# The last batch of a mixer kernel: only its last mixer in halves, and the router's mean summed by TensorE

## The chip, the cores and the metric

One core of a Trainium2 chip runs the whole kernel. The metric is device time in microseconds of one launch, the median over runs.

## The reference

The input x is 8 batches of 1024 tokens by 256 channels, float32. For each batch:

```python
n = layernorm(x)
logits = n @ gate_W                      # 4 mixers, the best 2 with softmax weights: comb
for m in 4 mixers:
    g, v, d = n @ Wg[m] + bg[m], n @ Wv[m] + bv[m], n @ Wd[m] + bd[m]
    h[m] = linear_scan(sigmoid(g) * tanh(v), a=0.001 + 0.998 * sigmoid(d))   # along the tokens
t = x + layernorm(sum_m comb[m] * h[m])
u = layernorm(t)
z = batchnorm(mean of u * ln_g + ln_b over the tokens)
expert, gate = argmax and max of softmax(z @ Wr + br)     # one of 8 experts per batch
y = (relu(u' @ W_down[expert] + b) @ W_up[expert] + b) * gate    # u' = u * ln_g + ln_b
out = t + layernorm(y)
```

(The reference's own names for the shapes of the expert part are larger; it runs on the same 8 batches.) The scan is serial over the 1024 tokens; everything that follows the mean over all tokens (the expert) needs the whole batch.

## The kernel before

Channels lie on the partitions for the products and scans, tokens for the normalisations. A batch has 8 planes (mixer m, half of the channels); a plane has 2 chunks of 512 tokens and 3 kinds (gate, decay, value), so a batch has 48 banks. Each bank is 6 float16 products of 128 x 512 (high and low parts of x and of the weights; `product`, L1196) into one of three PSUM banks, which ACT evacuates with sigmoid or tanh (`evacuate`, L535; L541 maps the decay). VectorE multiplies gate and value (L830), scans a plane (L806) and adds the mixers up (`combine`, L823) from transposed states: TensorE's float32 transposes `turn_h` (L1206). `a_moments`, `residual` and `t_moments` (statistics at L704) lead to t, with a power on POOL (L429) for each root; `scale_t` (L740, L743) gives factor and shift of each token, and the rows normalised by ACT (L571) or VectorE (L756) are turned by `turn_u` (L1159) and split into fp16 halves by ACT (`high_u`, L548, which also sums them over the tokens by accumulation) and VectorE (`low_u`, L863). `route_in`, `route` (L1216), `route_logits` and `route_pick` choose the expert; SP loads it (L313). `down` (L1226), `hidden_part`, `join_h`, `high_h`, `low_h` and `up` (L1235) are the expert; `y_moments`, `scale_y`, and `add_scaled` or ACT's `scale_rows` (L642) with `finish_late` (L947) end the batch.

The order of each engine is written out by hand. All engines run a loop over the batches: in the steady batch (`run`) the second part of the batch before (pv) is woven between the banks of this one (bt), and the normalisation, turning and gate products (L1175) of the next (nx) too. TensorE's order hangs on the bank number i. The last batch has an order of its own, `last`: all its planes are cut into halves of 512 tokens, first all 8 planes of the first half (banks 0 to 23), then of the second, and a scan of a second half starts from a column that is copied to `carry` (L810) after the first. Thus the statistics of the first half are done before the products end, and the tail behind the products serves the second half alone. Order of VectorE in the last batch: see `last` below. Engines wait on counting semaphores; a waiting instruction holds up all that is behind it on its engine.

## Time and profile before

| | |
|---|---|
| median of 3 runs | 722.65 us (722.2 to 724.97) |
| the profiled execution | 725.28 us, its span 723.5 us |
| busy: TensorE, VectorE, ACT, POOL | 90%, 83%, 64%, 16% of the span |
| mean granted TensorE clock | 0.952 |
| steady batch | 79.02 us (from transposes to the same transposes) |
| first product of the last batch to the end | about 148 us |

The span runs from the first to the last instruction of the profiled execution. Busy shares are means over stages that differ: TensorE is near full in the loop and mostly idle in the last 50 us.

### The profile page before, as it was taken

What the parts mean: (1) busy time and instruction counts of PE and PEld (TensorE: products, weight loads), DVE (VectorE), ACT (ScalarE), POOL (GpSimd) and SP (SyncE); (2) the same over time, 40 slices, a digit from 0 to 9 for tenths busy, and PEclk for the clock granted to TensorE, in tenths of its full rate; (3) what the DMA queues carried; (4) which work ended last, traced back from release to release, by engine and by line L of the source; (5) the groups of instructions that cost most, each with busy time, mean ns of one, the idle gap of its engine ahead of it and who ended that gap; (6) DMA issues with size and microseconds to landing.
All of it is one profiled execution on the core that took longest, in us unless ns stands there. A gap on an engine that the chain in (4) does not pass through costs nothing. (4 is left out here: it accounts for less than half of the span.)

```text
span 723.5 us, 11397 instructions
## 1 busy us (share of the span) xinstructions
PE 648.0 (90%) x3569; PEld 347.4 (48%) x3569; DVE 601.2 (83%) x1338; ACT 460.2 (64%) x819; POOL 118.4 (16%) x182
## 2 busy tenths in 40 slices
PE   3999989999999999999999999999999997698323
PEld 2455545555545555555545545455555554444211
DVE  7674999889997989889987989879988998677666
ACT  3748638875787558865887558854877566566203
POOL 2010032004310152006110241005200211001001
PEclk9989999999999999999999999999999999989655
DMA  8600130021202030101102030203000000000003
GB/s 228 182 1 0 59 117 1 1 69 40 79 1 70 3 119 2 41 30 64 55 1 70 5 118 1 70 1 117 2 0 12 31 30 0 12 0 1 0 25 103
DMA packets 34596, 31.87 MB, mean 44 GB/s; under 512 B 5814, under 2 KB 34522, under 8 KB 34522
## 3 DMA queue, kind: packets, MB, share of 16 engines
q1 hardware_dynamic: 34524, 31.00, 13.7%
q8 instruction: 35, 0.57, 0.3%
q14 instruction: 37, 0.30, 0.1%
HBM read 21.03 MB, written 8.39 MB: 41 GB/s over the span
## 5 line engine op out<-in xcount | busy, mean ns | idle before, releaser
L1196 PE MATMUL ps_main<-xh,w_hi 128*128 128x512 f16 x768 | 295.0, 384 | 4.8 <-ACT decay_s L535 3.3
L1196 PE MATMUL ps_main<-xh,w_lo 128*128 128x512 f16 x768 | 295.0, 384 | 0.0
L1196 PE MATMUL ps_main<-xl,w_hi 128*128 128x512 f16 x768 | 294.7, 384 | 0.0
L806 DVE TENSOR_TENSOR_SCAN hid<-decay_s,value_s 128x1024 f32<-128x1024 f32 (+1 forms) x64 | 138.1, 2158 | 6.7 <-DVE value_s L830 1.7
L535 ACT ACTIVATE value_s<-ps_main,vecs 128x512 f32<-128x512 f32 x128 | 88.7, 693 | 71.9 <-PE ps_main L1196 71.9
L535 ACT ACTIVATE decay_s<-ps_main,vecs 128x512 f32<-128x512 f32 x128 | 88.5, 691 | 65.0 <-PE ps_main L1196 60.5
L535 ACT ACTIVATE gate_s<-ps_main,vecs 128x512 f32<-128x512 f32 x128 | 88.0, 688 | 54.4 <-PE ps_main L1196 50.6
L1196 PEld LDWEIGHTS ps_main<-xl,w_hi 128*128 128x128 f16 x768 | 76.0, 99 | 93.1 <-issue 4.3
L1196 PEld LDWEIGHTS ps_main<-xh,w_hi 128*128 128x128 f16 x768 | 76.3, 99 | 91.1 <-ACT decay_s L535 4.3
L1196 PEld LDWEIGHTS ps_main<-xh,w_lo 128*128 128x128 f16 x768 | 75.9, 99 | 84.6 <-issue 3.8
L830 DVE TENSOR_TENSOR value_s<-gate_s,value_s 128x1024 f32<-128x1024 f32 (+1 forms) x72 | 79.2, 1100 | 16.8 <-ACT value_s L535 16.5
L823 DVE SCALAR_TENSOR_TENSOR mixed<-ps_aux,comb,mixed 128x256 f32<-128x256 f32 x192 | 77.5, 474 | 17.7 <-PE ps_aux L1206 16.9
L1206 PE MATMUL ps_aux<-ident,hid 128*128 128x128 f32 x512 | 66.9, 284 | 17.7 <-DVE hid L806 8.3
L1206 PEld LDWEIGHTS ps_aux<-ident,hid 128*128 128x128 f32 x512 | 60.6, 147 | 25.9 <-issue 14.5
L541 ACT ACTIVATE decay_s<-decay_s 128x1024 f32<-128x1024 f32 (+1 forms) x72 | 69.2, 961 | 0.0
L429 POOL TENSOR_TENSOR root_y<-root_in_y,neg_half 128x8 f32<-128x8 f32 (+1 forms) x9 | 13.5, 1496 | 273.0 <-DVE root_in_y L920 273.0
L1159 PE MATMUL ps_aux<-ident,normed 128*128 128x128 f32 x256 | 33.9, 283 | 25.9 <-DVE normed L756 22.3
L1159 PEld LDWEIGHTS ps_aux<-ident,normed 128*128 128x128 f32 x256 | 30.2, 146 | 32.0 <-DVE normed L756 12.7
L429 POOL TENSOR_TENSOR root_a<-root_in_a,neg_half 128x8 f32<-128x8 f32 (+1 forms) x9 | 16.9, 1877 | 119.1 <-DVE root_in_a L835 119.1
L429 POOL TENSOR_TENSOR root_t<-root_in_t,neg_half 128x8 f32<-128x8 f32 (+1 forms) x9 | 19.4, 2155 | 81.1 <-DVE root_in_t L856 81.1
L548 ACT ACTIVATE u_split<-ps_aux 128x512 f16<-128x512 f32 x32 | 18.8, 600 | 21.7 <-PE ps_aux L1159 21.7
L571 ACT ACTIVATE normed<-resid,shift_t,mul_by_t 128x256 f32<-128x256 f32 x56 | 30.4, 592 | 2.9 <-DVE shift_t L743 2.9
(162 smaller groups left out, 635.2 us busy)
## 6 DMA issues: line engine op xcount, KB each, us to landing
x_in<-in_L_attn_x SPq DMA_DIRECT2D x16, 512.0 KB, 4.4
resid<-in_L_attn_x SPq DMA_DIRECT2D x7, 1024.0 KB, 5.2
out<-resid SPq DMA_DIRECT2D x7, 1024.0 KB, 4.5
expert<-experts SPq DMA_DIRECT2D x8, 192.5 KB, 2.2
w_stage<-in_L_attn_Wg SPq DMA_DIRECT2D x4, 256.0 KB, 3.5
w_stage<-in_L_attn_Wd SPq DMA_DIRECT2D x4, 256.0 KB, 4.4
w_stage<-in_L_attn_Wv SPq DMA_DIRECT2D x4, 256.0 KB, 4.9
u_split<-in_L_ffn_W_down SPq DMA_DIRECT2D x4, 256.0 KB
```

What stands on the lines that cost most here:

```text
L429: pool.tensor_tensor(root[key][:, span(c)], root_in[key][:, span(c)], neg_half[:, span(c)], ALU.pow).then_inc(rooted, units(c))
L535: act.activation(staged(buf, pc, c), ps_main[:, i % BANKS], ACT.Tanh if kind == VALUE else ACT.Sigmoid, bias=vecs[:, col:col + 1], scale=Q ...
L541: act.activation(d, d, ACT.Copy, bias=0.001, scale=0.998).then_inc(decay_ready, 1)
L548: act.activation(uh[:, k, chunk(cc)], ps_aux[:, KT * cc + k], ACT.Copy, accum_out=u_sums[:, k, cc:cc + 1]).then_inc(uh_ready, 1)
L571: ins = act.activation(normed[:, t], rows[:, t], ACT.Identity, bias=shift[key][:, t:t + 1], scale=mul_by[key][:, t:t + 1])
L806: dve.tensor_tensor_scan(states(pc), staged(decay_s, pc, pc.c), staged(value_s, pc, pc.c), start, ALU.mult, ALU.add).then_inc(scanned, 1)
L823: ins = dve.scalar_tensor_tensor(mixed[:, t], ps_tok[:, t], comb[:, t, m:m + 1], mixed[:, t], ALU.mult, ALU.add)
L830: dve.tensor_tensor(v, staged(gate_s, pc, pc.c), v, ALU.mult).then_inc(input_ready, 1)
L1159: ins = pe.transpose(ps_aux[:, KT * cc + k, tile(t % (T // C))], normed[:, t, k * P:(k + 1) * P], ident[:])
L1196: ins = pe.matmul(ps_main[:, i % BANKS], w[:, 3 * m + kind, k, half * P:(half + 1) * P], v[:, bt.par, k, chunk(c)], start=(n == 0), stop=( ...
L1206: ins = pe.transpose(ps_tok[:, t, k * P:(k + 1) * P], state_tile(b, m, k, t), ident[:])
```

## The change

The last batch has six whole planes and only its last mixer (planes 6 and 7) in halves: pieces 6 and 7 are the first half, 8 and 9 the second, which start from the last column of the first half in `hid`. TensorE, ACT and VectorE follow the steady batch's bank numbers, without the work for a next batch. The statistics of both halves come after the last combine, interleaved: both a_moments, both residuals, both t_moments. The router's mean is no longer the sum that ACT accumulates; TensorE multiplies the rows of t with the factors of the tokens (one column) and adds the sum of the shifts with a matrix of ones (`sum_rows`), and `rows_in` adds up the two halves. ACT normalises the first half, VectorE the second. The diff, cut (removed lines of the long orders, which stand above, are left out):

```diff
@@ -242,7 +244,8 @@
 
         def pieces(b):
             if b.cut:
-                return [Piece(PLANES * c + p, p, c) for c in range(C) for p in range(PLANES)]
+                return ([Piece(p, p, None) for p in range(WHOLE)]
+                        + [Piece(WHOLE + KT * c + k, WHOLE + k, c) for c in range(C) for k in range(KT)])
             return [Piece(p, p, None) for p in range(PLANES)]
...
         def banks_before(pc):
-            return 3 * pc.q * (C if pc.c is None else 1)
+            return 3 * C * pc.q if pc.c is None else 3 * (C * WHOLE + pc.q - WHOLE)
...
         def staged(buf, pc, c):
 
-            return buf[:, pc.q % 2, tokens(c) if pc.c is None else chunk(pc.q // 2 % 2)]
+            return buf[:, pc.plane % 2, chunk(c) if c is not None else tokens(None)]
 
         def states(pc):
 
-            return hid[:, pc.q % 4, tokens(None) if pc.c is None else chunk(pc.q // 4 % 2)]
+            return hid[:, pc.plane % 4, tokens(pc.c)]
...
@@ -484,11 +483,11 @@
             def last(bt, pv):
                 power("a", a_root_in, a_root, pv)
                 power("t", t_root_in, t_root, pv)
-                power("a", a_root_in, a_root, bt, 0)
-                power("t", t_root_in, t_root, bt, 0)
                 power("y", y_root_in, y_root, pv)
-                power("a", a_root_in, a_root, bt, 1)
-                power("t", t_root_in, t_root, bt, 1)
+                for c in range(C):
+                    power("a", a_root_in, a_root, bt, c)
+                for c in range(C):
+                    power("t", t_root_in, t_root, bt, c)
                 for c in range(C):
                     power("y", y_root_in, y_root, bt, c)
...
                 fresh = i - banks_before(pc) < 3
-                behind = 3 if bt.cut and pc.q >= 2 else 1
-                if fresh and not (first and pc.q < 2) and not (bt.cut and pc.q in (2, 3)):
+                if fresh and not (first and pc.q < 2) and not pc.c:
                     if kind == GATE:
-                        act.wait_ge(input_ready, PLANES * bt.n + pc.q - behind)
+                        act.wait_ge(input_ready, PLANES * bt.n + pc.q - 1)
                     if kind == DECAY:
-                        act.wait_ge(scanned, PLANES * bt.n + pc.q - behind)
+                        act.wait_ge(scanned, PLANES * bt.n + pc.q - 1)
...
             def last(bt, pv):
...
                     if 19 <= i < 23:
                         normalise_t(pv, pair(i, 19))
                     if i in (23, 24):
                         high_u(pv, i - 23)
+                    if i == 25:
+                        shares(bt)
                     if i == 27:
                         router_sigmoids(pv)
...
+                    if 28 <= i < 32:
+                        start_mix(bt, pv, pair(i, 28))
+                    if i == 33:
+                        for c in range(C):
+                            hidden_part(pv, c)
+                    if i in (33, 34):
+                        high_h(pv, i - 33)
                     if i >= 44:
                         if i == 44:
                             act.wait_ge(y_scaled, pv.n + 1)
                         scale_rows(pair(i, 44))
                     evacuate(bt, i, bank, False)
 
...
+                normalise_t(bt, tiles(0))
+                high_u(bt, 0)
                 router_sigmoids(bt)
+                high_u(bt, 1)
                 for c in range(C):
                     hidden_part(bt, c)
                     high_h(bt, c)
...
-                if bt.cut and pc.c:
-                    dve.wait_ge(h_turned, turned(bt, pc.plane // KT, 0))
-                elif pc.q < 4 or bt.cut:
+                if pc.q < 4:
                     if not first:
-                        dve.wait_ge(h_turned, TURNS * bt.n - (C if pc.q % 4 < KT else 0))
+                        dve.wait_ge(h_turned, TURNS * bt.n - (C if pc.q < KT else 0))
                 else:
-                    dve.wait_ge(h_turned, turned(bt, pc.q // KT - 2, C - 1))
+                    dve.wait_ge(h_turned, turned(bt, pc.plane // KT - 2, C - 1))
                 start = 0.0
                 if pc.c:
-                    dve.wait_ge(carried, pc.plane + 1)
-                    start = carry[:, pc.plane:pc.plane + 1]
+                    dve.wait_ge(scanned, PLANES * bt.n + pc.q - KT + 1)
+                    start = hid[:, pc.plane % 4, CHUNK - 1:CHUNK]
                 dve.tensor_tensor_scan(states(pc), staged(decay_s, pc, pc.c), staged(value_s, pc, pc.c), start,
                                        ALU.mult, ALU.add).then_inc(scanned, 1)
-                if pc.c == 0:
-                    dve.wait_ge(scanned, PLANES * bt.n + pc.q + 1)
-                    dve.tensor_copy(carry[:, pc.plane:pc.plane + 1], states(pc)[:, CHUNK - 1:CHUNK]
-                                    ).then_inc(carried, 1)
...
+            def rows_in(b):
+
+                link = linker(route_link, ROUTE_LINKS * b.n)
+                dve.wait_ge(rows_summed, 1)
+                link(dve.tensor_reduce(z_mean[:, 0], ps_sums.rearrange("p c k -> p k c"), AX.X, ALU.add))
+                z_share(b, link)
+
             def last(bt, pv):
                 pcs = pieces(bt)
...
                 scan(pv, pieces(pv)[7])
                 combine(pv, 2)
                 combine(pv, 3)
                 a_moments(pv)
...
                 scan(bt, pcs[0])
                 residual(pv)
+                t_moments(pv)
                 scan(bt, pcs[1])
...
+                scale_t(pv)
                 scan(bt, pcs[2])
...
+                rank_mixers(bt)
+                low_u(pv)
+                weights_of(bt)
+                route_in(pv)
+                route_logits(pv)
+                route_pick(pv)
+                scan(bt, pcs[3])
+                scan(bt, pcs[4])
+                for c in range(C):
+                    join_h(pv, c)
+                low_h(pv)
+                combine(bt, 1)
                 scan(bt, pcs[5])
...
+                y_moments(pv)
                 scan(bt, pcs[6])
...
+                scale_y(pv)
                 scan(bt, pcs[7])
                 scan(bt, pcs[8])
...
+                combine(bt, 2)
                 scan(bt, pcs[9])
...
+                combine(bt, 3)
+                for c in range(C):
+                    a_moments(bt, c)
+                for c in range(C):
+                    residual(bt, c)
+                for c in range(C):
+                    t_moments(bt, c)
+                for c in range(C):
+                    scale_t(bt, c)
+                    dve.wait_ge(t_scaled, done(bt, c))
+                    dve.tensor_reduce(shift_sum[:, c:c + 1], shift["t"][:, span(c)], AX.X, ALU.add
+                                      ).then_inc(shift_summed, 1)
+                normalise("t", t_rows(bt), t_scaled, u_late, bt, 1)
+                rows_in(bt)
                 low_u(bt, 0)
...
                 route_logits(bt)
                 route_pick(bt)
+                low_u(bt, 1)
                 finish_late(pv, None)
                 for c in range(C):
                     join_h(bt, c)
...
             def turn_u(pv, c=None):
-                pe.wait_ge(u_ready, done(pv, c))
+                if pv.cut and c == C - 1:
+                    pe.wait_ge(u_late, 1)
+                else:
+                    pe.wait_ge(u_ready, done(pv, c))
...
+            def sum_rows(b, c):
+
+                pe.wait_ge(t_scaled, done(b, c))
+                pe.wait_ge(shift_summed, c + 1)
+                for k in range(KT):
+                    for t in tiles(c):
+                        pe.matmul(ps_sums[:, c, k:k + 1], t_rows(b)[:, t, k * P:(k + 1) * P], mul_by["t"][:, t:t + 1],
+                                  start=(t == tiles(c)[0]), stop=False)
+                    ins = pe.matmul(ps_sums[:, c, k:k + 1], ones[:], shift_sum[:, c:c + 1], start=False, stop=True)
+                if c == C - 1:
+                    ins.then_inc(rows_summed, 1)
+
             def last(bt, pv):
                 for i, bank in enumerate(banks(bt)):
                     finish_h(bt, pv, i)
...
+                    if i in (22, 24):
+                        c = (i - 22) // 2
+                        pe.wait_ge(combined, summed_up(pv, 3, c))
+                        turn_u(pv, c)
                     if i == 27:
                         route(pv)
...
+                        for c in range(C):
+                            low_u_done(pv, c)
+                            turn_h(bt, 0, c)
+                    if i == 33:
+                        pe.wait_ge(mix_started, done(bt))
+                        down(pv)
                     if i == 34:
...
+                        for c in range(C):
+                            pe.wait_ge(h_ready, done(pv, c))
+                            turn_h(bt, 1, c)
                     if i == 37:
...
+                        for c in range(C):
+                            pe.wait_ge(combined, summed_up(bt, 1, c))
+                            up(pv, c)
                     if i == 47:
                         pe.wait_ge(y_normed, T // C)
...
+                        turn_h(bt, 2, 0)
                     product(bt, i, bank, False)
                 pe.wait_ge(y_normed, T)
...
+                turn_h(bt, 2, 1)
+                for c in range(C):
+                    pe.wait_ge(combined, summed_up(bt, 2, c))
+                    turn_h(bt, 3, c)
+                sum_rows(bt, 0)
+                pe.wait_ge(combined, summed_up(bt, 3, 0))
+                turn_u(bt, 0)
+                sum_rows(bt, 1)
+                route(bt)
+                pe.wait_ge(combined, summed_up(bt, 3, 1))
                 turn_u(bt, 1)
...
                 down(bt)
                 for c in range(C):
                     up(bt, c)
```

## Rows read from the trace of the kernel before

**Rows 1.** Stretches: length, busy us (instructions) per engine, clock, DMA share, GB/s.

```profile
670.70:703.80 33.10, 7.59 (x34) 6.06 (x34) 22.82 (x75) 3.97 (x13) 2.01 (x2) 0.56 0.02 6
```

**Rows 2.** TensorE by time, last batch: start, length, instruction, count, idle before.

```profile
582.40 1.91 PE L1206 MATMUL ps_aux<-ident,hid 128*128 128x128 f32 x16
...
606.88 1.94 PE L1206 MATMUL ps_aux<-ident,hid 128*128 128x128 f32 x8 [3.57 <-DVE hid L806]
608.61 0.63 PE L1196 MATMUL ps_main<-xh,w_hi 128*128 128x512 f16 x1
...
616.37 1.94 PE L1159 MATMUL ps_aux<-ident,normed 128*128 128x128 f32 x16 [1.65 <-ACT normed L571]
...
631.86 1.94 PE L1206 MATMUL ps_aux<-ident,hid 128*128 128x128 f32 x8 [4.78 <-DVE hid L806]
...
661.15 0.46 PE L1196 MATMUL ps_main<-xh,w_hi 128*128 128x512 f16 x1 [2.34 <-ACT decay_s L535]
...
670.79 1.09 PE L1206 MATMUL ps_aux<-ident,hid 128*128 128x128 f32 x8 [0.43 <-ACT x_in L642]
```

**Rows 3.** TensorE by time, steady batch; last, the stretch of its gate products.

```profile
495.16 1.91 PE L1206 MATMUL ps_aux<-ident,hid 128*128 128x128 f32 x16
...
529.32 1.06 PE L1159 MATMUL ps_aux<-ident,normed 128*128 128x128 f32 x8 [0.27 <-ACT normed L571]
...
538.64 0.39 PE L1216 MATMUL ps_misc<-z_wr,ones 128*128 128x8 f32 x2 [0.91 <-DVE z_wr L874]
...
574.18 1.91 PE L1206 MATMUL ps_aux<-ident,hid 128*128 128x128 f32 x16
...
569.48:570.31 0.83, 0.82 (x32) 0.82 (x31) 1.00 0.00 0
```

**Rows 4.** VectorE by time, steady batch; last, a half scan of the last batch.

```profile
526.33 0.17 DVE L743 SCALAR_TENSOR_TENSOR shift_t<-moments_t,mul_by_t 128x8 f32<-128x8 f32 x1
526.44 2.48 DVE L764 TENSOR_TENSOR xl<-ps_aux,xh 128x512 f16<-128x512 f32 x4
...
561.67 2.74 DVE L704 BATCH_NORM_STATS2 stats_y<-ps_aux 128x6 f32<-128x256 f32 x8
...
611.33 1.22 DVE L806 TENSOR_TENSOR_SCAN hid<-decay_s,value_s 128x512 f32<-128x512 f32 x1
```

**Rows 5.** ACT by time, last batch: two rows of y.

```profile
664.42 1.01 ACT L642 ACTIVATE x_in<-ps_aux,add_y,mul_by_y 128x256 f32<-128x256 f32 x2
```

**Rows 6.** VectorE by time, last batch, behind the products.

```profile
680.85 1.66 DVE L823 SCALAR_TENSOR_TENSOR mixed<-ps_aux,comb,mixed 128x256 f32<-128x256 f32 x4 [2.12 <-PE ps_aux L1206]
682.55 1.40 DVE L704 BATCH_NORM_STATS2 stats_a<-mixed 128x6 f32<-128x256 f32 x4
...
686.10 1.67 DVE L849 SCALAR_TENSOR_TENSOR x_in<-mixed,root_a,x_in 128x256 f32<-128x256 f32 x4
687.80 1.41 DVE L704 BATCH_NORM_STATS2 stats_t<-x_in 128x6 f32<-128x256 f32 x4
...
691.67 1.38 DVE L756 TENSOR_SCALAR normed<-x_in,mul_by_t,shift_t 128x256 f32<-128x256 f32 x4
695.83 0.16 DVE L870 TENSOR_TENSOR z_mean<-u_sums 128x2 f32<-128x2 f32 x1 [2.78 <-ACT u_split L548]
```

**Rows 7.** POOL by time, same stretch.

```profile
690.23 1.01 POOL L429 TENSOR_TENSOR root_t<-root_in_t,neg_half 128x4 f32<-128x4 f32 x1 [4.25 <-DVE root_in_t L856]
```

**Rows 8.** The line L1251: durations ns min/median/max; then a stretch of time.

```profile
L1251 PEld LDWEIGHTS ps_misc<-vecs,u_split x32: 190/192/333, 43.8 to 47.8; 128*128 128x128 f32 x32
L1251 PE MATMUL ps_misc<-vecs,u_split x32: 167/250/352, 44.0 to 47.8; 128*128 128x1 f32 x32
...
46.00:48.00 2.00, 2.00 (x15) 2.00 (x15) 1.90 (x2) 0.00 (x0) 0.00 (x0) 0.73 0.04 8
```

**Rows 9.** TensorE by time, last batch: router product, first down product.

```profile
696.96 0.60 PE L1216 MATMUL ps_misc<-z_wr,ones 128*128 128x8 f32 x2 [1.89 <-DVE z_wr L874]
703.86 1.46 PE L1226 MATMUL ps_aux<-u_split,expert 128*128 128x512 f16 x3 [6.29 <-DMA expert<-experts]
```

More of the change, by code:

```diff
@@ L40, in mixer_kernel @@
     PLANES = M * KT
+    WHOLE = PLANES - KT
     EVAC = PLANES * 3 * C
@@ L169, in mixer_kernel @@
         scanned = sem("scanned")
-        carried = sem("carried")
+        shift_summed, rows_summed, u_late = sem("shift_summed"), sem("rows_summed"), sem("u_late")
         h_turned = sem("h_turned")
@@ L646, in last @@
                 for i, bank in enumerate(banks(bt)):
-                    if i == 3:
-                        shares(bt)
-                    if i in (17, 18):
-                        start_mix(bt, pv, pair(i, 17))
                     if 19 <= i < 23:
@@ L669, in last @@
                     evacuate(bt, i, bank, False)
-                for c in range(C):
-                    high_u(bt, c)
+                normalise_t(bt, tiles(0))
+                high_u(bt, 0)
                 router_sigmoids(bt)
+                high_u(bt, 1)
                 for c in range(C):
@@ L1089, in last @@
                 a_moments(pv)
-                weights_of(bt)
                 scan(bt, pcs[0])
                 residual(pv)
+                t_moments(pv)
                 scan(bt, pcs[1])
-                t_moments(pv)
+                scale_t(pv)
                 scan(bt, pcs[2])
-                scale_t(pv)
-                for q in (3, 4):
-                    scan(bt, pcs[q])
-                combine(bt, 1, 0)
-                scan(bt, pcs[5])
+                rank_mixers(bt)
                 low_u(pv)
+                weights_of(bt)
                 route_in(pv)
-                scan(bt, pcs[6])
                 route_logits(pv)
-                combine(bt, 2, 0)
                 route_pick(pv)
-                scan(bt, pcs[7])
-                scan(bt, pcs[8])
-                combine(bt, 3, 0)
-                a_moments(bt, 0)
-                scan(bt, pcs[9])
-                residual(bt, 0)
-                scan(bt, pcs[10])
+                scan(bt, pcs[3])
+                scan(bt, pcs[4])
                 for c in range(C):
@@ L1116, in last @@
                 low_h(pv)
-                t_moments(bt, 0)
-                scan(bt, pcs[11])
+                combine(bt, 1)
+                scan(bt, pcs[5])
                 y_moments(pv)
-                scale_t(bt, 0)
-                scan(bt, pcs[12])
+                scan(bt, pcs[6])
                 scale_y(pv)
-                scan(bt, pcs[13])
-                scan(bt, pcs[14])
-                scan(bt, pcs[15])
-                for m in (1, 2, 3):
-                    combine(bt, m, 1)
-                a_moments(bt, 1)
-                low_u(bt, 0)
-                residual(bt, 1)
-                t_moments(bt, 1)
-                scale_t(bt, 1)
-                normalise("t", t_rows(bt), t_scaled, u_ready, bt, 1)
-                route_in(bt)
-                low_u(bt, 1)
+                scan(bt, pcs[7])
+                scan(bt, pcs[8])
+                combine(bt, 2)
+                scan(bt, pcs[9])
+                combine(bt, 3)
[12 more added lines that the diff above has]
+                rows_in(bt)
+                low_u(bt, 0)
                 route_logits(bt)
                 route_pick(bt)
+                low_u(bt, 1)
                 finish_late(pv, None)
@@ L1345, in last @@
                     if i == 27:
                         route(pv)
-                    if i == 29:
-                        pe.wait_ge(combined, summed_up(bt, 2, 0))
-                        turn_h(bt, 3, 0)
+                        for c in range(C):
[4 more added lines that the diff above has]
+                        down(pv)
                     if i == 34:
-                        pe.wait_ge(combined, summed_up(bt, 3, 0))
-                        down(pv)
+                        for c in range(C):
+                            pe.wait_ge(h_ready, done(pv, c))
+                            turn_h(bt, 1, c)
@@ L1353, in last @@
                     if i == 37:
-                        pe.wait_ge(h_ready, done(pv))
-                        turn_h(bt, 0, 1)
-                    if i == 39:
-                        pe.wait_ge(mix_started, done(bt, 1))
-                        up(pv)
+                        for c in range(C):
+                            pe.wait_ge(combined, summed_up(bt, 1, c))
+                            up(pv, c)
                     if i == 47:
                         pe.wait_ge(y_normed, T // C)
-                        turn_u(bt, 0)
+                        turn_h(bt, 2, 0)
@@ L1362, in last @@
                     product(bt, i, bank, False)
                 pe.wait_ge(y_normed, T)
-                turn_h(bt, 1, 1)
-                for m in (2, 3):
-                    pe.wait_ge(combined, summed_up(bt, m - 1, 1))
-                    turn_h(bt, m, 1)
+                turn_h(bt, 2, 1)
[4 more added lines that the diff above has]
+                pe.wait_ge(combined, summed_up(bt, 3, 0))
```

43 lines of the change are left out of this document (10 added, 33 removed).

## The prediction, on record before the changed kernel ran

> **What bounds the kernel now.** I read the table of stretches first [rows 1], then TensorE's instructions in order of time, first of the last batch and then of the steady one, and then VectorE's in order of time to the end. In the last batch TensorE stands still four times between the first and the last product: 3.57, 1.65, 4.78 and 2.34 us [rows 2]; the reader is to see that VectorE's half scans release two of them and ACT the other two. After such a stop it also runs at the lower clock for a while: the 8 transposes at 606.88 take 1.94 us, as long as 16 elsewhere (1.91 at 582.40). In the steady batch the same engine waits 0.27 and 0.91 us [rows 3]. Once the products are done, the time goes to one chain: transposes, sums and statistics of the last half on VectorE, the router, the load of the expert. That is 33 us with TensorE busy for 7.6 of them at a clock of 0.56, that is mostly at 1.2 GHz [rows 1]. The end follows 19.64 us after the first "down" product (703.86 to 723.5).
>
> **The change, part by part.** All times are those of the profiled execution, span 723.5 us.
>
> *1. The last batch in the steady order.* The steady batch begins with 16 transposes at 495.16 and the last one with the same at 574.18, so a steady event at t becomes t + 79.02 [rows 3]. Two things of the steady batch are missing in the last one: the x transposes at bank 12 (16 transposes; 8 take 1.73 us at half clock from 606.88 to 608.61, so 16 take 1.73 at full clock) and VectorE's low halves of x (2.48 us) [rows 2, 4]. The first makes TensorE early at bank 22, but there it waits for ACT's normalised rows, which wait for VectorE's shift_t at 526.33 + 79.02 = 605.35; nothing of the missing x work lies ahead of that on VectorE, except its own x statistics, and those are made good by TensorE's bank 5, where the statistics' successor waits anyway. So from bank 22 on the template holds: that wait grows from 0.27 to about 2.0, and the 0.91 for the router stays. The 2.48 us of low halves come off behind shift_t, where VectorE then waits for ACT's u rows; worth nothing. At the end the 32 gate products go (0.83) [rows 3] and 8 transposes of mixer 2 come (0.87). The last product ends at 574.18 + 79.02 = 653.2. Now it is at 670.2 (670.79 less 0.43 of waiting, less the 0.2 by which a modelled end lies behind the next start) [rows 2]. Gain on this part: 17.0.
>
> *2. The last mixer in halves.* A bank takes (582.40 − 574.18 − 1.73)/5 = 1.30, so bank 44 is full at 653.2 − 3 × 1.30 − 0.87 = 648.4. VectorE's own times: scan 5 ends at 561.67 + 79.02 = 640.7; y statistics 2.74 plus 1.2 of small operations to 644.6; a half scan 1.22 with its multiply 0.68 and gaps 2.0 [rows 4] to 646.6; scale_y 0.7 to 647.3; the second half scan to 649.3; the third waits for ACT, which has put two rows of y ahead of bank 44 (0.9 for two) [rows 5], and ends at 651.4. The transposes of mixer 2 are done at 652.0, its first half is combined in 1.66 [rows 6] to 653.7. The second half is turned once ACT has scaled all eight y rows, at 653.9, and combined from 654.9 to 656.6. Fourth half scan to 658.6. The copies of a carried state go (a small operation after each half scan); the second halves read it from hid instead, which I take as nothing, between 0 and 0.15 us for each of two. Mixer 3: first half to 660.3; the second is turned from 658.6, after 2.6 idle us of TensorE, so at half clock in 1.97, and combined to 662.3.
>
> *3. Both halves of the statistics behind that.* Statistics of a half: from 687.80 to POOL's start at 690.23, 2.35 without the hand-over [rows 6, 7]; twice 4.7, to 667.0. POOL's root (1.01) [rows 7] lies beside the other half's statistics. Residual 1.70 and a small operation each (686.10 to 687.80) [rows 6]: 3.5, to 670.5. Statistics of t, again 4.7, to 675.2. scale_t 0.4 and the new reduction of four shifts (a small operation with its wait, 0.25): 675.8. Today this path serves one half and takes 680.85 + 1.66 = 682.5 to 691.67, 9.2 us; it becomes 13.5, but begins 20.2 earlier. VectorE's scaling of the second half's rows (1.38) goes beside TensorE's sums; if those were gone, it would show.
>
> *4. The mean by TensorE.* Each half: 8 products of 128 x 128 float32 rows by one column plus 2 with ones, 10 calls. The before kernel has this very form once: 16 calls at L1251 are 32 recorded pairs, so 2 instructions a call, 20 a half; their loads start from 43.8 to 47.8, 0.13 apart, and the clock falls to 0.73 in the second stretch, so they do not keep it up [rows 8]. What is not shown is their pace at half clock throughout. From below: 0.109 each at full clock (1.73/16). From above: load and multiply one after the other, 0.333 + 0.352 = 0.685, the longest of that line. I take 0.216, the pace of the 8 float32 transposes at half clock [rows 2], since these too are set by loads of 128 columns, and TensorE will have been idle from 660.6 to 675.8. Then 4.3 a half. They stand in one queue: sums 0 (675.8 to 680.1), u transposes 0 (1.73, to 681.9; its rows come from ACT at about 677.7, hidden), sums 1 (to 686.2, result 0.2 later). VectorE's reduction of the sums starts at 686.4; its counterpart, the addition of the two ACT sums, starts now at 695.83 [rows 6]. Shift: −9.4.
> The Trainium skill, "FP8 and Floating Point Precision", section "TensorE Precision Notes", says that true float32 is four passes through the array. The 32 pairs for 16 calls say two; by the page the sums would be 40 passes a half, and its result is among the rivals.
>
> *5. From there to the end.* Now 8.03 from the addition to the first down product (695.83 to 703.86) [rows 6, 9]. In it the router product of 0.60 lies beneath 1.28 us of low halves of u; half 0's take the place of half 1's, length unchanged. Half 1's go behind the router's pick. Half 1 is turned by TensorE after the router product (1.73), turned to fp16 by ACT after the two sigmoids (1.4), then its low halves on VectorE end 6.4 after the addition: 1.6 us of slack to 8.03. The previous batch's last sum and its 1 MB store move behind that, 2.8 us on VectorE until 9.2, before join_h is wanted at 10.6; the output store it shares the queue with comes 14 us later. ACT's new normalisation of half 0 has an idle ACT. So down begins at 694.5 and the end is 694.5 + 19.6 = 714.1.
>
> **Sum.** −17.0 for the products, +7.6 behind them (from 670.2 to 695.83 was 25.6, from 653.2 to 686.4 is 33.2): −9.4. The profiled execution took 725.28 with span 723.5; it would take 715.9. Against the median of the runs, 722.65, this gives 713.2.
>
> **Rivals.**
> *A. The sums at full clock.* Sums and transposes follow one another without a gap, and that might raise the clock. For: in the last batch the clock comes back while transposes and products run. Against: it fell under the same one-column form at L1251 [rows 8]. 20 × 0.109 a half and 0.87 for the transposes: 5.1 less, 708.1.
> *B. Calls not overlapped.* The router's lone call, same form with 8 columns, took 0.60 for its two instructions at half clock [rows 9]; all 20 calls at that price 12.0 instead of 8.6: 716.6. Against: at L1251 they overlap.
> *C. The clock falls at the longer wait of bank 22.* A stop of 2.34 us was followed by slow products, one of 1.65 was not [rows 2]; 2.0 lies between. About eight products at 0.43 instead of 0.216 or the transposes in their place, 1.7 us, as behind 661.15; it is late for the router too and carried on: 715.
> *D. Four passes.* 40 more passes × 0.216 = 8.6: 721.9, no change.
> *E. The steady order is not reached*, because VectorE, not TensorE, sets the pace of the last batch from bank 27 on, with whole scans ahead of the router's work. For: VectorE is busy 83% over all. Against: that very order runs in each steady batch with 1.2 us of waits on TensorE. If half of the 17.0 is lost: 721.8.
> *F. Slower.* The 16 products of a half accumulate into two PSUM columns; if each must be finished before the next load begins, an instruction costs 0.685, 40 of them 27.4 instead of 8.6: 732. It decides from (8.6 + 9.4)/40 = 0.45 us an instruction on. Against: L1251's pairs accumulate likewise and come 0.13 us apart (4.0/31).
>
> **Chances.** Forecast 0.52, A 0.15, B 0.10, C 0.15, D 0.03, E 0.03, F 0.02. Predicted is 713.2. From A to B and C is 708.1 to 716.6; my sums of VectorE's gaps can be off by 1 to 2 us either way, so 708.0 to 718.5. What a measurement can tell from no change is 0.5%, 3.6 us, so faster means below 719.0: the forecast, A, B and C, 0.92; D and E are within, 0.06; F is slower, 0.02.
>
> **What would show it.** Part 1: the first 16 transposes of the last batch still at 574.2, one wait of about 2 us at bank 22 and one near 0.9 before the router product, last product near 653.2. Part 2: the last combine ends near 662.3. Part 3: the first sum product starts near 675.8. Part 4: 20 instructions take 4.3 us, clock 0.50, the reduction at 686.4. Part 5: 8.0 to down, 19.6 to the end. The prediction is wrong if the waits at 3.57 to 4.78 come back, if the sums' spacing is far from 0.216, or if the reduction is not what releases z_mean's chain.

## The result

| | before | changed |
|---|---|---|
| median over runs | 723.81 us (4 runs, 722.2 to 725.46) | 714.38 us (4 runs, 712.26 to 714.8) |
| profiled execution, span | 725.28, 723.5 | 712.26, 710.5 |
| last batch: from its first 16 transposes to the end | 149.3 us | 138.2 us |
| mean granted clock | 0.952 | 0.964 |

The ratio is 0.9864, 95% interval 0.983 to 0.9897: 1.4% faster, with 713.2 forecast for 714.4. The two profiled executions differ by 1.9 us ahead of the change already (574.18 against 572.30 for the first transposes of the last batch [rows 3]); I therefore measure all profiles from there, the "last batch". It is 11.1 us shorter; 9.4 were forecast. Part of that surplus belongs to the two executions compared: a third profile of the old order (e5_mean below) has 147.8 us there, for the same work at another clock.

TensorE of the changed kernel by time, as [rows 2, 3, 9] have it for before:

```profile
572.30 1.91 PE L1202 MATMUL ps_aux<-ident,hid 128*128 128x128 f32 x16
...
606.17 1.06 PE L1155 MATMUL ps_aux<-ident,normed 128*128 128x128 f32 x8 [1.72 <-ACT normed L569]
...
615.49 0.39 PE L1215 MATMUL ps_misc<-z_wr,ones 128*128 128x8 f32 x2 [0.91 <-DVE z_wr L868]
...
656.63 1.06 PE L1202 MATMUL ps_aux<-ident,hid 128*128 128x128 f32 x8 [2.94 <-DVE hid L800]
672.55 1.83 PE L1335 MATMUL ps_misc<-mul_by_t,x_in 128*128 128x1 f32 x8 [14.86 <-DVE shift_sum L1126]
...
674.67 1.85 PE L1335 MATMUL ps_misc<-mul_by_t,x_in 128*128 128x1 f32 x8
...
676.81 1.95 PE L1155 MATMUL ps_aux<-ident,normed 128*128 128x128 f32 x8
678.55 1.71 PE L1335 MATMUL ps_misc<-mul_by_t,x_in 128*128 128x1 f32 x8
...
683.99 0.60 PE L1215 MATMUL ps_misc<-z_wr,ones 128*128 128x8 f32 x2 [1.17 <-DVE z_wr L868]
...
690.84 1.46 PE L1225 MATMUL ps_aux<-u_split,expert 128*128 128x512 f16 x3 [4.46 <-DMA expert<-experts]
```

In place of the four stops of 3.57, 1.65, 4.78 and 2.34 us, 12.3 in all, there are two, 1.72 (for ACT's rows, as the 1.65 before) and 0.91. The last product comes 17.35 us earlier in the last batch (17.0 forecast): 9.7 of them are stops, and about 6 the transposes and products that ran at half clock behind the old stops (two sets of 8 transposes in 1.73 instead of 0.87 us, 21 products 0.43 apart instead of 0.216). Behind the products the reader is to see the queue of four pieces of work: sums of half 0, transposes of u, sums of half 1, router product. A set of 20 instructions takes 4.26 us (672.55 to 676.81). VectorE in the same stretch, against [rows 6]:

```profile
649.94 1.66 DVE L813 SCALAR_TENSOR_TENSOR mixed<-ps_aux,comb,mixed 128x256 f32<-128x256 f32 x4 [0.58 <-PE ps_aux L1202]
652.85 1.66 DVE L813 SCALAR_TENSOR_TENSOR mixed<-ps_aux,comb,mixed 128x256 f32<-128x256 f32 x4 [1.26 <-PE ps_aux L1202]
...
656.40 3.20 DVE L813 SCALAR_TENSOR_TENSOR mixed<-ps_aux,comb,mixed 128x256 f32<-128x256 f32 x8
659.52 1.39 DVE L700 BATCH_NORM_STATS2 stats_a<-mixed 128x6 f32<-128x256 f32 x4
...
672.25 0.16 DVE L1126 TENSOR_REDUCE shift_sum<-shift_t 128x1 f32<-128x4 f32 x1
673.05 0.17 DVE L736 TENSOR_SCALAR mul_by_t<-root_t 128x4 f32<-128x4 f32 x1 [0.64 <-POOL root_t L428]
...
682.85 0.16 DVE L1081 TENSOR_REDUCE z_mean<-ps_misc 128x2 f32<-128x4 f32 x1 [7.96 <-PE ps_misc L1337]
```

It combines the last mixer to 659.60, has both halves' factors and shifts by 673.4, is done with its rows at 674.9 and then waits 7.96 us for TensorE's sums. In the stretches (columns as [rows 1]) the clock had fallen before the sums began, and stayed at 0.50 under them:

```profile
658.00:661.00 3.00, 0.00 (x0) 0.00 (x0) 2.97 (x10) 0.00 (x0) 0.00 (x0) 0.67 0.00 0
661.00:672.00 11.00, 0.00 (x0) 0.00 (x0) 10.48 (x47) 0.00 (x0) 3.26 (x3) 0.50 0.00 1
...
676.00:680.00 4.00, 4.00 (x21) 4.00 (x21) 0.00 (x0) 1.38 (x4) 0.00 (x0) 0.50 0.00 0
```

### The profile page after: what moved, and what is told of

It reads as the page before. It is cut to its first block and busy times, and to the rows that moved or that the text cites. A ratio compares the mean times of both kernels' runs of the same rounds, so it can differ in the third digit from the quotient of the medians.

```text
span 710.5 us, 11434 instructions
## 1 busy us (share of the span) xinstructions
PE 646.5 (91%) x3609; PEld 351.4 (49%) x3609; DVE 597.7 (84%) x1320; ACT 459.0 (65%) x813; POOL 123.3 (17%) x182
## 5 line engine op out<-in xcount | busy, mean ns | idle before, releaser
L800 DVE TENSOR_TENSOR_SCAN hid<-decay_s,value_s 128x1024 f32<-128x1024 f32 (+1 forms) x64 | 144.6, 2260 | 6.7 <-DVE value_s L820 1.4
L533 ACT ACTIVATE gate_s<-ps_main,vecs 128x512 f32<-128x512 f32 x128 | 88.1, 688 | 54.8 <-PE ps_main L1192 52.8
L1202 PE MATMUL ps_aux<-ident,hid 128*128 128x128 f32 x512 | 62.3, 274 | 8.2 <-DVE hid L800 2.9
L1202 PEld LDWEIGHTS ps_aux<-ident,hid 128*128 128x128 f32 x512 | 57.4, 141 | 15.0 <-issue 9.1
L1155 PE MATMUL ps_aux<-ident,normed 128*128 128x128 f32 x256 | 35.5, 290 | 13.7 <-DVE normed L752 10.0
L569 ACT ACTIVATE normed<-x_in,shift_x,mul_by_x 128x256 f32<-128x256 f32 x56 | 30.6, 603 | 0.0
```

The lines of the kernel that those rows point to most:

```text
L533: act.activation(staged(buf, pc, c), ps_main[:, i % BANKS], ACT.Tanh if kind == VALUE else ACT.Sigmoid, bias=vecs[:, col:col + 1], scale=Q ...
L569: ins = act.activation(normed[:, t], rows[:, t], ACT.Identity, bias=shift[key][:, t:t + 1], scale=mul_by[key][:, t:t + 1])
L800: dve.tensor_tensor_scan(states(pc), staged(decay_s, pc, pc.c), staged(value_s, pc, pc.c), start, ALU.mult, ALU.add).then_inc(scanned, 1)
L1155: ins = pe.transpose(ps_aux[:, KT * cc + k, tile(t % (T // C))], normed[:, t, k * P:(k + 1) * P], ident[:])
L1202: ins = pe.transpose(ps_tok[:, t, k * P:(k + 1) * P], state_tile(m, k, t), ident[:])
```

## The experiments

"Ratio" is to the kernel before, timed beside each; "last batch" is the profile's, from the first 16 transposes to the end of the span.

| kernel | median us | ratio (95%) | last batch | z_mean's chain starts, from the same point |
|---|---|---|---|---|
| before, two profiles | 723.81; 724.33 | 1.0013 (0.9999 to 1.0026) | 149.3; 149.1 | 121.65; 121.4 |
| changed, again (a0_after) | 713.87 | 0.9862 (0.984 to 0.9884) | 138.1 | 110.5 |
| e1_accum | 710.04 | 0.9806 (0.9783 to 0.9828) | 134.6 | 107.0 |
| e2_double | 722.43 | 0.9976 (0.9963 to 0.9989) | 146.7 | 119.1 |
| e3_warm | 709.67 | 0.9817 (0.9798 to 0.9837) | 135.2 | 107.6 |
| e4_whole | 718.37 | 0.993 (0.9909 to 0.9951) | 143.3 | 115.7 |
| e5_mean | 723.9 | 0.9998 (0.9986 to 1.0011) | 147.8 | 120.6 |
| e6_inturn | 713.83 | 0.986 (0.9837 to 0.9883) | 138.6 | 110.9 |
| b1_best | 708.55 | 0.9781 (0.9759 to 0.9803) | 133.0 | 105.6 |
| b2_best | 707.5 | 0.9785 (0.9768 to 0.9802) | 132.6 | 105.0 |

**a0_after, the changed kernel again.**

> The changed kernel again, as the neighbour of the next three. Theory T (the gain is the steady order with its two missing waits, and the tail's length is VectorE's chain plus TensorE's queue of sums): last product of the last batch 77 us after its first, span near 712, 9 to 11 us below the kernel before. Its runs so far scatter from 712.3 to 714.8; if a fall of the clock at bank 22 (a wait of 1.72 us in the profile) or at the last transposes of h makes that, a slower profile shows products 0.43 apart there.

The last batch is 138.1 against 138.2: it repeats. The 2.6 us between the two spans (713.1, 710.5) lie ahead of it, where the clock of the first batches differs. First this run's two stretches, then those of the first profile of the changed kernel:

```profile
30.00:60.00 30.00, 29.04 (x143) 15.38 (x141) 22.79 (x29) 16.31 (x26) 3.53 (x11) 0.89 0.04 15
...
90.00:120.00 30.00, 28.12 (x146) 15.33 (x145) 28.69 (x57) 17.61 (x29) 7.94 (x12) 0.94 0.23 72
```

```profile
30.00:60.00 30.00, 29.04 (x150) 15.32 (x149) 23.79 (x31) 17.15 (x28) 4.56 (x11) 0.94 0.05 18
...
90.00:120.00 30.00, 28.13 (x153) 15.41 (x152) 28.84 (x62) 19.78 (x33) 7.96 (x12) 1.00 0.22 72
```

So the scatter between runs is not at bank 22, as I had thought possible.

**e1_accum, the new order with the old mean.** The edit, the main lines (besides, the sums of the shifts go, and ACT makes the high half of the second half's rows ahead of the router's sigmoids):

```diff
...
-                rows_in(bt)
                 low_u(bt, 0)
+                route_in(bt)
+                low_u(bt, 1)
...
-                sum_rows(bt, 0)
                 turn_u(bt, 0)
-                sum_rows(bt, 1)
-                route(bt)
                 turn_u(bt, 1)
+                route(bt)
```

> The new order alone: the mean comes again from ACT's accumulation, so the 40 sum products and the two reductions of shifts go, TensorE turns both halves and then does the router product. Theory T: the second half's rows are ready at 674.9 in the time of the changed kernel's profile, turned by 677.9 at half clock, split by ACT by 679.2; z_mean's chain starts at 679.2 instead of 682.85, so 3.5 us faster than the changed kernel (0.5%). Rival (the sums take work off the path, since they need no normalised rows and no ACT): slower than the changed kernel by 1 us or more.

Its last batch is 3.6 shorter than the changed kernel's (3.5 expected), and the intervals of the two ratios do not meet. TensorE turns all 16 blocks at once at 676.21:

```profile
676.21 3.65 PE L1152 MATMUL ps_aux<-ident,normed 128*128 128x128 f32 x16 [16.56 <-ACT normed L569]
681.75 0.59 PE L1212 MATMUL ps_misc<-z_wr,ones 128*128 128x8 f32 x2 [1.89 <-DVE z_wr L868]
...
680.39 0.19 ACT L546 ACTIVATION_READ_ACCUMULATOR u_split<-ps_aux 128x1 f32 x1
680.62 0.16 DVE L860 TENSOR_TENSOR z_mean<-u_sums 128x2 f32<-128x2 f32 x1 [1.01 <-ACT u_split L546]
```

The chain starts when ACT's last accumulator is read. So the new order with the old mean gains 14.7 us of the last batch, and the mean by TensorE gives 3.6 back. This profile's own last transposes of h were slow (1.71 us for 8 instead of 1.06), which hides some of it: from the end of the last combine to the start of the chain it is 23.25 us in the changed kernel and 19.27 here, a price of 4.0.

**e2_double, the sums made twice.**

```diff
-                for k in range(KT):
+                for k in [*range(KT), *range(KT)]:
```

> Each half's sums are made twice (the second set starts anew and gives the same numbers): 40 products more. Theory T: all of TensorE's queue between the first scale and the reduction is on the path at 0.215 us an instruction, so 8.6 us slower than the changed kernel. Rival (the sums overlap with VectorE's work and only the last half counts): 4.3 us. Rival (clock returns under a longer stretch of them): 3 to 5 us.

8.5 us slower than the changed kernel (8.6 expected): every one of the sums' instructions is on the path, and neither smaller rival holds. VectorE's wait for them doubles from 7.96, and the clock did not come back under 18.6 us of sums and transposes without a gap:

```profile
692.99 0.16 DVE L1081 TENSOR_REDUCE z_mean<-ps_misc 128x2 f32<-128x4 f32 x1 [16.49 <-PE ps_misc L1337]
...
680.00:686.00 6.00, 6.00 (x31) 6.00 (x30) 0.00 (x0) 1.38 (x4) 0.00 (x0) 0.50 0.00 0
```

**e3_warm, TensorE kept busy ahead of the sums.**

```diff
+                pe.wait_ge(main_read, EVAC * (bt.n + 1))
+                for j in range(66):
+                    pe.matmul(ps_main[:, j % BANKS], w_hi[:, 0, 0, 0:P], xh[:, bt.par, 0, chunk(0)],
+                              start=True, stop=True)
                 sum_rows(bt, 0)
```

> 66 added products of 128x512 into ps_main after the last transposes of h, 14.3 us of TensorE's idle time at full clock, whose results nobody reads; they end shortly before the sums start. Theory T (sums at half clock, 0.215 each, are paced by the clock): the 40 sums take 0.109 each and the transposes between half as long, z_mean's chain starts 5.0 us earlier; 5 us faster than the changed kernel. Rival (a one-column product costs 0.2 us at any clock): no change. Rival (one-column products let the clock fall again midway, as the similar ones at the start of the kernel did): 2.5 to 4 us faster.

The last batch is 2.9 to 3.0 us shorter than the changed kernel's, so the third of the three expectations holds. The first 20 instructions take 2.22 us (672.70 to 674.92), 0.111 each; in the second set the clock falls under them:

```profile
657.67 14.41 PE L1375 MATMUL ps_main<-xh,w_hi 128*128 128x512 f16 x66
672.70 1.02 PE L1335 MATMUL ps_misc<-mul_by_t,x_in 128*128 128x1 f32 x8 [0.62 <-DVE shift_sum L1126]
...
674.92 1.07 PE L1155 MATMUL ps_aux<-ident,normed 128*128 128x128 f32 x8
675.83 1.59 PE L1335 MATMUL ps_misc<-mul_by_t,x_in 128*128 128x1 f32 x8
...
677.70 1.85 PE L1335 MATMUL ps_misc<-mul_by_t,x_in 128*128 128x1 f32 x8
...
672.00:675.00 3.00, 2.38 (x22) 2.33 (x22) 2.22 (x11) 2.07 (x4) 1.01 (x1) 1.00 0.00 0
675.00:678.00 3.00, 3.00 (x21) 3.00 (x20) 0.04 (x1) 1.27 (x4) 0.00 (x0) 0.66 0.00 0
678.00:681.00 3.00, 1.97 (x10) 1.89 (x9) 0.85 (x5) 0.00 (x0) 0.00 (x0) 0.50 0.00 0
```

Twenty one-column products, 8 transposes of 128 columns and more one-column products, without a gap between them, did not hold the clock. At L1251 before [rows 8] the one-column products stand alone, directly behind a run of full products and without a stop, and there too the clock falls: it is 1.00 from 44 to 46 us, 0.97 from 46 to 47 and 0.50 from 47 to 48. So the one-column form is enough to let it fall. The prediction's rival A (the clock rises under the sums) is answered by this, by e2_double and by the stretches of the changed kernel.

**e4_whole, no halves at all.**

```diff
-            if b.cut:
-                return ([Piece(p, p, None) for p in range(WHOLE)]
-                        + [Piece(WHOLE + KT * c + k, WHOLE + k, c) for c in range(C) for k in range(KT)])
...
-                scan(bt, pcs[7])
-                scan(bt, pcs[8])
                 combine(bt, 2)
-                scan(bt, pcs[9])
+                scan(bt, pcs[7])
```

> The changed kernel with all eight planes of the last batch whole: the last mixer's two scans are not cut, VectorE does scan 6, combine of mixer 2, scan 7, combine of mixer 3. Theory T: products end at the same place of the last batch; the last scan (1.2 multiply, 2.3 scan) and both halves' transposes of mixer 3 then stand behind one another, where the cut kernel had a half scan (2.0) there: 2 to 3 us slower than the changed kernel. Rival (halves cost more than they hide, since the steady order alone makes the gain): equal within 1 us.

5.2 us slower in the last batch, more than the 2 to 3 expected. The lines:

```profile
650.18 1.09 PE L1197 MATMUL ps_aux<-ident,hid 128*128 128x128 f32 x8 [1.08 <-ACT x_in L637]
...
659.61 3.40 PE L1197 MATMUL ps_aux<-ident,hid 128*128 128x128 f32 x16 [5.36 <-DVE hid L797]
...
657.17 2.29 DVE L797 TENSOR_TENSOR_SCAN hid<-decay_s,value_s 128x1024 f32<-128x1024 f32 x1
661.64 2.83 DVE L810 SCALAR_TENSOR_TENSOR mixed<-ps_aux,comb,mixed 128x256 f32<-128x256 f32 x7 [2.18 <-PE ps_aux L1197]
```

The whole scan is 1.6 longer than scan 9's half; the whole scan 6 stands ahead of scale_y, so ACT's rows of y and the transposes of mixer 2 come 1.3 later; and nothing of mixer 3 has been turned ahead: TensorE stops for 5.36, turns 16 blocks at half clock, and VectorE waits 2.18 for the first eight. These three, 1.6, 1.3 and 2.18, make 5.1. I had counted only the first.

**e5_mean, the old order with the new mean.** In the kernel before, shifts are reduced behind each scale_t, VectorE's low halves of the second half go behind the router's pick, ACT's high half of it behind the router's sigmoids, and TensorE does:

```diff
-                turn_u(bt, 1)
-                route(bt)
+                sum_rows(bt, 0)
+                sum_rows(bt, 1)
+                route(bt)
+                turn_u(bt, 1)
```

> The kernel before, with nothing changed but the mean: reductions of the shifts, both halves' sums on TensorE (the first in the idle time behind the last transposes of h), rows_in, and the second half turned behind the router product. Theory T: the second half's sums start at 691.9, take 4.3 at half clock, z_mean's chain starts 0.6 later than before (696.4), and gets 0.6 back since no low halves lie between it and the logits: no change, within 1 us of the kernel before. Rival (the mean by TensorE is a part of the gain, as it needs no normalised rows): 2 to 4 us faster.

No change: 0.9998. The sums of the second half take the place of normalising, turning and evacuating it:

```profile
608.50 1.06 PE L1228 MATMUL ps_aux<-ident,hid 128*128 128x128 f32 x8 [3.58 <-DVE hid L809]
...
691.96 1.84 PE L1358 MATMUL ps_misc<-mul_by_t,x_in 128*128 128x1 f32 x8 [7.16 <-DVE shift_sum L1100]
...
696.39 0.16 DVE L1094 TENSOR_REDUCE z_mean<-ps_misc 128x2 f32<-128x4 f32 x1 [3.29 <-PE ps_misc L1360]
```

Its last batch is 147.8 and not 149.3 because TensorE's clock stayed up behind the first stop, of 3.58 us, there (the 8 transposes at 608.50 are followed by products 0.90 later, 1.73 at that place before), which is no effect of the edit: nothing of the edit lies ahead of that place. Counted from the turning at bank 23 (616.37 [rows 2], 616.40) the chain's start is 0.5 later and the end 0.1 later. The rival, 2 to 4 us faster, does not hold.

**e6_inturn, the halves' statistics one after the other.** VectorE's order; POOL's roots change places likewise:

```diff
...
                 for c in range(C):
                     a_moments(bt, c)
-                for c in range(C):
                     residual(bt, c)
-                for c in range(C):
                     t_moments(bt, c)
-                for c in range(C):
                     scale_t(bt, c)
```

> The changed kernel with the statistics of the last batch's halves one after the other instead of interleaved (on VectorE and POOL). Theory T: VectorE stands still for POOL's roots, about 1.2 us three or four times, and ends its chain near 4.5 us later; but the first half's sums start 3.5 us earlier and TensorE's queue of sums hides it: the chain of z_mean starts within 1 us of the changed kernel's. Rival (the interleaving is what shortens the tail): 3.5 to 4.5 us slower.

The last batch is 0.4 to 0.5 us longer, the ratio 0.986 against 0.9862. VectorE's chain ends 5 us later, and it costs nothing that the timing can tell:

```profile
656.75 1.94 PE L1198 MATMUL ps_aux<-ident,hid 128*128 128x128 f32 x8 [2.95 <-DVE hid L799]
669.72 1.84 PE L1331 MATMUL ps_misc<-mul_by_t,x_in 128*128 128x1 f32 x8 [11.03 <-DVE shift_sum L1122]
...
673.98 1.95 PE L1151 MATMUL ps_aux<-ident,normed 128*128 128x128 f32 x8
678.90 1.84 PE L1331 MATMUL ps_misc<-mul_by_t,x_in 128*128 128x1 f32 x8 [2.98 <-DVE shift_sum L1122]
...
658.73 1.66 DVE L812 SCALAR_TENSOR_TENSOR mixed<-ps_aux,comb,mixed 128x256 f32<-128x256 f32 x4 [0.57 <-PE ps_aux L1198]
...
683.34 0.16 DVE L1080 TENSOR_REDUCE z_mean<-ps_misc 128x2 f32<-128x4 f32 x1 [3.29 <-PE ps_misc L1333]
```

The first half's sums and transposes run before the second half's factors are there. The interleaving alone is worth nothing as long as TensorE's sums follow it. In this run the transposes at 656.75 took 1.94, in the changed kernel 1.06, after the same stop of 2.95 (2.94): and VectorE then waits 0.57 for them, which is more than the 0.4 to 0.5 by which the batch is longer. Eight profiles of the new order have this stop (e4_whole has 5.36 in its place); in two of them the clock fell (e1_accum in part), though the stops are alike.

**b1_best and b2_best, versions for speed.** The new order, ACT's mean, the first half one step ahead, added products before the turning and before "down":

```diff
...
+                residual(bt, 0)
+                t_moments(bt, 0)
+                residual(bt, 1)
+                scale_t(bt, 0)
+                t_moments(bt, 1)
+                scale_t(bt, 1)
...
+                idle_products(bt, 62)
                 turn_u(bt, 0)
...
                 turn_u(bt, 1)
                 route(bt)
+                idle_products(bt, 26)
```

> A version for speed: the changed kernel's order with the mean by ACT's accumulation, the first half ahead by one step (both a_moments, residual 0, t_moments 0, residual 1, scale 0, t_moments 1, scale 1), and 62 and 26 added products of TensorE before the turning of the first half and before the down products, whose results nobody reads. Theory T: the first half is turned under the statistics of the second, both turnings take 0.9 instead of 1.75, z_mean's chain starts 5.5 to 6 us earlier than the changed kernel's, the down products take half their time (0.9 off the path): 6 to 7 us faster than the changed kernel, 3 us faster than the new order with ACT's mean. Rival (added products delay the work behind them, or the clock falls in the gaps all the same): no faster than the new order with ACT's mean.

133.0: 5.1 shorter than the changed kernel, 1.6 than e1_accum, less than the 6 to 7 and 3 expected; and since its ratio's interval overlaps that of e1_accum, the rival (no faster than the new order with ACT's mean) is not excluded by the timing. The down products take half their time, but start 0.7 later after the chain's start, behind added products that ran at half clock themselves for their first 3 us (granted clock 0.50 from 682 to 685, 1.00 from 686 on); the second turning came after a gap of 1.99 and mostly at half clock. What the order one step ahead gives and what the added products give was not separated. In b2_best the counts are 66, 7 between the turnings, and 27:

> The version for speed with its added products spread anew: 66 before the first half's turning (it stood idle for 1.26 us there), 7 between the two turnings (1.99 us idle, after which the second turning ran at half clock), 27 before the down products. Theory T (the clock falls in gaps of 2 to 3 us in all and the added products must fill them): both turnings take 0.9, z_mean's chain starts 0.9 earlier in the last batch than in the version before, 27 products at full clock take 5.8 us and end before the expert is there, the down products start 8.0 after the chain's start instead of 8.7: last batch 131.5 us instead of 133.0. Rival (the clock falls in spite of them): 133 again.

```profile
674.28 1.06 PE L1152 MATMUL ps_aux<-ident,normed 128*128 128x128 f32 x8 [0.38 <-ACT normed L569]
675.18 1.67 PE L1329 MATMUL ps_main<-xh,w_hi 128*128 128x512 f16 x7
677.33 1.06 PE L1152 MATMUL ps_aux<-ident,normed 128*128 128x128 f32 x8 [0.48 <-DVE normed L752]
...
680.43 0.39 PE L1212 MATMUL ps_misc<-z_wr,ones 128*128 128x8 f32 x2 [2.03 <-DVE z_wr L868]
680.67 7.67 PE L1329 MATMUL ps_main<-xh,w_hi 128*128 128x512 f16 x27
688.18 1.89 PE L1222 MATMUL ps_aux<-u_split,expert 128*128 128x512 f16 x8
...
679.00:680.00 1.00, 0.00 (x0) 0.00 (x0) 0.60 (x4) 0.26 (x2) 0.00 (x0) 1.00 0.00 0
681.00:682.00 1.00, 1.00 (x5) 0.31 (x3) 0.93 (x4) 0.00 (x0) 0.00 (x0) 0.53 0.00 0
```

Both turnings are at full clock now, the chain starts 0.6 earlier (0.9 expected), but behind the wait of 2.03 us for the router's input the clock falls again: it is still 1.00 within the wait and 0.53 from 681 to 682, under the first added products. The 27 take 7.5 us instead of 5.8, and down is late as before. 132.6: 0.4 shorter and not 1.5; between b1 and b2 the timing tells nothing. Both are faster than the changed kernel (intervals apart) and have the lowest medians of all; against e1_accum the intervals overlap.

**b0_before, the kernel before once more.**

> The kernel before once more, for a second profile. Theory T (the scatter of 3 us between runs lies in short stretches of half clock, at the start and after each long wait of TensorE in the last batch, and not in the work): the last batch takes 147.8 to 149.3 us from its first 16 transposes, stops of about 3.6, 1.65, 4.8 and 2.35 us at the same places, and differences from the first profile are multiples of a stretch of products 0.43 apart. Rival (another source): the stops themselves differ by over 1 us.

149.1, and stops of 3.57, 1.65, 4.78 and 2.33 at the same places. Its span of 721.3 is 2.2 below the first profile's, and 1.96 of it lies ahead of the last batch: the clock was 0.94 from 30 to 60 us and 1.00 from 90 to 120 us, against 0.89 and 0.94 in the first profile.

## Why the prediction was right

*Part 1, right.* From the first transposes of the last batch, the last product was forecast to have been issued after 79.0; it is 78.7 (a modelled end at 651.13 less 0.16). The one wait at bank 22 was forecast as 2.0 and is 1.72, the router's 0.91 is 0.91. None of the nine profiles of the new order has a slow transpose or product behind that wait: rival C did not come, nor E, since beside these two no stop is left before the last bank. e1_accum shows that the new order, without the new mean, makes more than the whole gain.

*Part 2, right but for one term.* Last combine after 88.1 forecast, 87.3 measured. Of these 0.8, 0.35 come from part 1. The clock at the last transposes of h makes most of the rest: I put it at half (1.97 and a wait of 0.3 for VectorE), and it was still full (1.06, no wait) after a stop of 2.94; e6_inturn has it the other way, with a wait of 0.57. That halving the last mixer pays was not priced by me; e4_whole puts it at 5.2 us.

*Part 3, right, 0.6 too long.* From the last combine to the first sum 13.5 forecast, 12.95 measured: each of the four statistics of a half is 2.25 (659.52 to 661.77) and not 2.35. I had read it up to the start of POOL's root, while VectorE itself goes on sooner; before the change too it goes on after 2.26 (682.55 to 684.81). Doing both halves behind the products was expected to cost 4.3 us more than one half, and the interleaving was counted as hiding POOL's roots; e6_inturn shows that those did not matter.

*Part 4, right, but the choice behind it was not priced.* Taken 0.216 an instruction, measured 0.213 (4.26/20); 10.6 forecast for the queue, 10.3 from 672.55 to 682.85. e2_double shows it all on the path, e3_warm that the clock sets it (0.111 at full). Rivals B, D and F are refuted by the spacing: 0.43 a call against 0.60, 20 instructions a half and not 40, 0.213 an instruction and not 0.45. The 0.216 was borrowed from the float32 transposes, and that it fits is shown for these two forms alone; float16 products of 8 columns with loads of 128 columns come 0.026 apart at full clock [rows 3], the float32 one-column products 0.111. The Trainium skill, "FP8 and Floating Point Precision", section "TensorE Precision Notes", counts four passes for true float32. The trace records two instruction pairs a call, each of them over four times as long as one float16 pair; how many passes lie in a pair no run here shows. What is refuted is rival D's price, 40 recorded instructions a half. The forecast took the mean by TensorE as given and did not ask what ACT's sum would cost in the new order: e1_accum shows that this half of the change costs 3.6 to 4.0 us, so the whole change is faster in spite of it.

*Part 5, right.* From the chain's start to down 7.99 (8.03 forecast), from there to the end 19.66 (19.64).

*The sum.* 9.4 forecast and 11.1 in the profiles: 0.35 from part 1, 0.45 more from part 2, 0.55 from part 3, 0.3 from part 4. The medians differ by 9.4 (9.8 by the ratio) and not by 11.1. That lies within the interval, 7.5 to 12.3 us, and fits the clock's scatter: e5_mean's execution of the old order has 1.5 us less in the last batch than the profile before. That the medians meet the forecast to the tenth is luck: the four differences have the same sign and make 1.65, and the scatter happens to offset them. What stays open is why the clock of the first batches, the one behind the first stop of the old order and the one at the last transposes of the new differ between executions of the same work.

## What to carry to other kernels

In the kernel before, cutting the whole last batch in halves to shorten the tail was bought with stops in the stage that had been full, and they cost more than the tail gave: count the stops of the busiest engine in the last batch against those in a steady one before adding to the tail's parallelism, and try cutting only the last stage (that gave 5.2 us here). A reduction moved to an idle engine is only free if it leaves the path; here the 40 one-column products of both halves, at a fallen clock, took 3.6 to 4.0 us longer than normalising, turning and accumulating the same rows, and with one half behind the products (e5_mean) the two ways were equal. An interleaving that fills one engine's gaps is worth nothing when a second engine's queue behind it is longer. A change of two parts is to be forecast part by part: the order alone would have been the better change.

## What the runs showed of the hardware

A stream of one-column float32 products with their loads, without a gap, did not hold the clock. At L1251 of the kernel before, 32 of them behind full products, it fell from 1.00 to 0.50 at 47 us; in e3_warm, with 8 transposes among them, it was 1.00 from 672 to 675, 0.66 from 675 to 678 and 0.50 after, and in e2_double it stayed at 0.50 through 18.6 us of them. Such a product with its load takes 0.111 us an instruction at full clock and 0.213 at half, two instructions a call. Standing still for 1.7 us did not lower the clock, in nine profiles. Longer stops went both ways: after 2.95 us it fell in e6_inturn and not in the changed kernel, and after 3.57 us in the kernel before and not, after 3.58, in e5_mean. So the length of a stop alone did not decide it. Added products of 128x512 in 14.4 us of idle time held it at 1.00 and cost VectorE's chain beside them nothing: the first sum starts 100.28 us into the last batch with them and 100.25 without.
